# Starting twelve expert blocks ahead of the final block table, earlier row loads, and two PSUM banks each for turned rows and output

## What is computed

```python
x = x + attn(layernorm(x))              # causal self-attention, 16 heads of 8
x = x + xattn(layernorm(x), ctx, ctx)   # cross-attention without a softmax, own layernorm on its result
x = x + ffn(layernorm(x))

def ffn(x):                             # 8 experts, 128 -> 512 -> 128
    assign = argmax(x @ centroids.T)    # one expert for each token
    xn = xhat * ln_g[e] + ln_b[e]
    h = relu(xn @ w1[e].T + b1[e])
    y = x + h @ w2[e].T + b2[e]
    a = sigmoid((x @ centroids.T)[e])
    return a * y + (1 - a) * x          # for the token's expert e
```

## Time and profile before

| what | value |
|---|---|
| median of 3 runs | 640.61 us (639.78 to 641.74) |
| the profiled execution's own time | 648.02 us |
| its span in the profile | 646.2 us |
| TensorE busy | 553.8 us (86%) |
| VectorE busy | 516.4 us (80%) |
| POOL busy | 486.3 us (75%) |
| ScalarE busy | 429.3 us (66%) |
| mean granted TensorE clock | 0.954 of full speed |

### The profile page before, as it was taken

The page is one execution under the profiler, slowest core; times in us unless marked ns, Lnnn a source line. Parts: engine busy times, 40 slices in busy tenths (PEclk is TensorE's granted clock), DMA queues, the critical chain, the costliest instruction groups (busy, mean ns, idle before and its releaser), DMA issues. The chain is left out here.

```text
span 646.2 us, 24863 instructions
## 1 busy us (share of the span) xinstructions
PE 553.8 (86%) x7908; PEld 421.4 (65%) x7940; DVE 516.4 (80%) x1852; ACT 429.3 (66%) x1127; POOL 486.3 (75%) x891
## 2 busy tenths in 40 slices
PE   1647999999999999999999999986329989899993
PEld 0434676766666666666666666654219989898893
DVE  1567799899999999999998999887557767676673
ACT  1534777877787877778787777763217777677771
POOL 1412478888888889888888888787826888887885
PEclk9877999999999999999999999999559999999998
DMA  8300112311221131111112111100021222221220
GB/s 156 96 8 26 44 44 63 91 52 52 69 85 52 56 95 55 52 56 50 36 40 65 37 36 40 41 24 20 18 66 52 70 59 65 61 70 52 65 63 9
DMA packets 55183, 35.35 MB, mean 55 GB/s; under 512 B 14977, under 2 KB 50434, under 8 KB 55057
## 3 DMA queue, kind: packets, MB, share of 16 engines
q1 hardware_dynamic: 49584, 24.16, 14.1%
q0 software_dynamic: 4320, 8.66, 3.9%
q10 hardware_dynamic: 1152, 0.94, 0.5%
HBM read 24.46 MB, written 9.74 MB: 53 GB/s over the span
## 5 line engine op out<-in xcount | busy, mean ns | idle before, releaser
L1753 POOL DMA_INDIRECT out<-yo,rb x71 | 74.3, 1046 | 23.1 <-issue 11.7
L962 ACT ACTIVATE prob<-quad 128x1024 f32<-128x1024 f32 x64 | 62.1, 1021 | 35.1 <-PE quad L679 35.1
L869 PE MATMUL quad<-w,hT 128*128 x568 | 78.0, 281 | 6.5 <-DVE yb L1556 5.0
L946 ACT ACTIVATE ex<-qk,cf 128x512 f32<-128x512 f32 x128 | 81.9, 718 | 0.0
L1712 POOL DMA_INDIRECT expert_rows<-pay,sli x64 | 65.7, 1026 | 20.1 <-issue 15.5
L1279 DVE TENSOR_REDUCE mx<-quad 128x16 f32<-128x1024 f32 x64 | 75.2, 1216 | 5.2 <-PE quad L644 4.6
L869 PEld LDWEIGHTS quad<-w,hT 128*128 128x128 f32 x568 | 69.8, 193 | 9.9 <-issue 9.3
L1747 POOL TENSOR_SCALAR bs<-rb 128x128 f32<-128x128 f32 x71 | 58.7, 826 | 10.5 <-DMA rb<-expert_rows 6.8
L1538 DVE TENSOR_SCALAR xh<-rb 128x128 f32<-128x128 f32 x71 | 28.7, 404 | 40.2 <-DMA rb<-expert_rows 25.7
L679 PE MATMUL quad<-ex,qk 32*64 32x256 f32 x1024 | 47.3, 396 | 4.4 <-issue 4.0
L1071 ACT ACTIVATE xhT<-quad,gb 128x128 f32<-128x128 f32 x71 | 32.5, 458 | 24.9 <-PE quad L844 18.3
(11 more groups left out here) (220 smaller groups left out, 1625.0 us busy)
## 6 DMA issues: line engine op xcount, KB each, us to landing
rb<-expert_rows SPq DMA_DIRECT2D x71, 68.0 KB
xin<-in_x SPq DMA_DIRECT2D x32, 128.0 KB, 2.5
cin<-in_ctx SPq DMA_DIRECT2D x32, 128.0 KB, 3.1
xr<-in_x SPq DMA_DIRECT2D x32, 128.0 KB, 2.2
w<-in_w1t SPq DMA_DIRECT2D x8, 256.0 KB, 3.5
w<-in_w2t SPq DMA_DIRECT2D x8, 256.0 KB, 3.4
out<-yo,rb POOLq DMA_INDIRECT x71
expert_rows<-pay,sli POOLq DMA_INDIRECT x64
```

The source lines that it names most:

```text
L869: last = mm(M[1][:, 0:D], hT[u][:, c, :], w2[:, bass.ds(e, 1), c, :], start=c == 0, stop=c == FC - 1)
L946: act(ex[g.par][:, i, :, :].rearrange("p a t -> p (a t)"), qk[g.par][:, :, :].rearrange("p a t -> p (a t)"), ACT.Copy, scale=own4[:, i:i + ...
L962: act(prob[g.par][:, 2 * h_:2 * h_ + 2, :], quad[:, 2 * h_:2 * h_ + 2, :], ACT.Exp).then_inc(*ac_a.done(f"e{h_}"))
L1753: v.indirect_dma_start(out=o_rows, out_offset=bass.IndirectOffsetOnAxis(ap=number, axis=0), in_=yo[b.c % 4][:, :], in_offset=None, bounds_ ...
```

## The change

- Row loads: x of group g is loaded in round g of SP's program, ctx in round g + 2 and the residual in round g + 3. `late_loads` keep their rounds.
- After `counted` of group 11 the counts are kept (`te`). 12 groups of 256 tokens hold at least 12 full blocks of 128. In round 33 VectorE computes a table of the first NB1 = 12 blocks from them (`early_table`), all full ones, and signals `s_tab` the first time. The preparations stand in round 9.
- SP fetches blocks 0 to 7 after its last row load, once the early table and the scatters of the first 12 groups are there. All eight pad writes are then on SP, followed by the fetches of blocks 8 to 11; from block 12 on it waits for the pads, the final table and all scatters.
- `rows_in` of blocks 0 and 1 is in VectorE's round 37; TensorE does `transposed` of 0 and 1 and `hidden` of 0 in round 38, after `ranks` of group 30 and before that of group 31.
- The final table leaves out the blocks already used and is computed in ten pieces in VectorE's blocks 1 to 5 (`last_table`), with the running sum as one masked reduction.
- Turned rows have banks 0 and 1, outputs banks 4 and 5. `transposed` and `second` lose their waits for the block before; `hidden` always waits for `act_xT` and `second` for `dve_relu`.

```diff
@@ -150,6 +150,9 @@
     NG = NT // J
     CAP = T + P
     NBLK = NT + E - 1
+    NB1, GT = 12, 12
+    NB2 = NBLK - NB1
+    assert RB <= NB1 and NB1 * P <= GT * TG - E * (P - 1)
     x_rows = x.rearrange("b s d -> (b s) d")
     c_rows = ctx.rearrange("b s d -> (b s) d")
     o_rows = out.rearrange("b s d -> (b s) d")
...
@@ -310,6 +325,7 @@
         side = es.enter_context(nc.psum_tensor("side", [P, 4, 512], FP32))
         bank = [quad[:, i, :] for i in range(4)] + [side[:, i, :] for i in range(4)]
         M = bank[0:2]
+        XT, YB = bank[0:2], bank[4:6]
         HT = [bank[2:4], bank[6:8]]
         def stage_steps(name, pieces):
...
@@ -504,24 +523,14 @@
                              ).then_inc(d_c[g.par], 16)
             def one(g):
-                stage(g, 6, load_ctx)
-                stage(g, 7, load_again)
-                stage(g, 4, load_x)
+                stage(g, 2, load_ctx)
+                stage(g, 3, load_again)
+                stage(g, 0, load_x)
             rounds(nc.sync, one, early=late_loads)
             sp.wait_ge(s_padt, 1)
             sp.dma_start(rows[E * CAP:E * CAP + P, :], padt[:, :]).then_inc(d_pad, 16)
-            sp.wait_ge(s_pads, 1)
-            for e in range(E // 2):
-                at = nc.sync.value_load(pri[0:1, e:e + 1], min_val=0, max_val=(e + 1) * CAP - P)
-                sp.dma_start(rows[bass.ds(at, P), :], padt[:, :]).then_inc(d_pad, 16)
-            sp.wait_ge(d_pad, 16 * (E + 1))
-            sp.wait_ge(s_tab, 1)
-
-            sp.wait_ge(d_s[0], 16 * J * ((NG + 1) // 2))
-            sp.wait_ge(d_s[1], 16 * J * (NG // 2))
-
             def fetch(b):
                 if b.c >= RB:
...
@@ -530,7 +539,24 @@
                 at = nc.sync.value_load(bti[0:1, 1, bass.ds(b.n, 1)], min_val=0, max_val=E * CAP)
                 sp.dma_start(rb[b.c % RB][:, :], rows[bass.ds(at, P), :]).then_inc(d_rb[b.c % RB], 16)
-            for c in range(NBLK):
+
+            sp.wait_ge(s_tab, 1)
+            sp.wait_ge(d_s[0], 16 * J * ((GT + 1) // 2))
+            sp.wait_ge(d_s[1], 16 * J * (GT // 2))
+            for c in range(RB):
+                fetch(Block(c))
+            sp.wait_ge(s_pads, 1)
+            for e in range(E):
+                at = nc.sync.value_load(pri[0:1, e:e + 1], min_val=0, max_val=(e + 1) * CAP - P)
+                sp.dma_start(rows[bass.ds(at, P), :], padt[:, :]).then_inc(d_pad, 16)
+            for c in range(RB, NB1):
+                fetch(Block(c))
+
+            sp.wait_ge(d_pad, 16 * (E + 1))
+            sp.wait_ge(s_tab, 2)
+            sp.wait_ge(d_s[0], 16 * J * ((NG + 1) // 2))
+            sp.wait_ge(d_s[1], 16 * J * (NG // 2))
+            for c in range(NB1, NBLK):
                 fetch(Block(c))
             for i in range(4):
...
@@ -827,21 +853,19 @@
                 stage(g, 2, values)
                 stage(g, 4, weighted, 1)
-            rounds(nc.tensor, one)
-
-
-            wait(pe, dv_r, NG - 1, "tot")
-
             def expert(b):
+
+                if b.c == NB1:
+                    pe.wait_ge(s_tab, 2)
                 return nc.tensor.value_load(bti[0:1, 0, bass.ds(b.n, 1)], min_val=0, max_val=E - 1)
             def transposed(b):
+
                 if b.c < 4:
                     wait_b(pe, "dve_xh", b.n)
-                wait_b(pe, "act_xT", b.n - 1)
-                tr(M[0][:, 0:P], xh[b.c % 2][:, :], identf).then_inc(*ffn["pe_xT"].done("pe_xT"))
+                tr(XT[b.c % 2][:, 0:P], xh[b.c % 2][:, :], identf).then_inc(*ffn["pe_xT"].done("pe_xT"))
             def hidden(b):
...
@@ -850,7 +874,7 @@
                 if b.c < 2:
                     wait_b(pe, "act_w1", b.n)
-                if b.c == NBLK - 1:
+                else:
                     wait_b(pe, "act_xT", b.n)
                 for c in range(FC):
                     last = mm(HT[u][c // 2][:, (c % 2) * P:(c % 2 + 1) * P], w1b[u][:, c * P:(c + 1) * P],
...
@@ -862,35 +886,33 @@
                 u = b.c % 2
                 wait_b(pe, "act_relu", b.n)
-                if b.c == 0:
-                    wait_b(pe, "dve_relu", b.n)
-                wait_b(pe, "dve_yb", b.n - 1)
+                wait_b(pe, "dve_relu", b.n)
                 for c in range(FC):
-                    last = mm(M[1][:, 0:D], hT[u][:, c, :], w2[:, bass.ds(e, 1), c, :],
+                    last = mm(YB[u][:, 0:D], hT[u][:, c, :], w2[:, bass.ds(e, 1), c, :],
                               start=c == 0, stop=c == FC - 1)
                 last.then_inc(*ffn["pe_y"].done("pe_y"))
+            def first_blocks(i):
+
+                if i == TOTAL - 2:
+                    transposed(Block(0))
+                    transposed(Block(1))
+                    hidden(Block(0))
+
+            rounds(nc.tensor, one, early=first_blocks)
+
+
             pe.wait_ge(s_tab, 1)
-
...
-            transposed(Block(0))
-            transposed(Block(1))
-            steps([Block(c) for c in range(NBLK + 1)])
+            e1 = expert(Block(0))
+            transposed(Block(2))
+            for c in range(1, NBLK + 1):
+                if c < NBLK:
+                    hidden(Block(c))
+                second(Block(c - 1), e1)
+                if c < NBLK:
+                    e1 = expert(Block(c))
+                if c + 2 < NBLK:
+                    transposed(Block(c + 2))
         @block.scalar
...
@@ -1058,17 +1080,13 @@
             ac.wait_ge(d_late, 16 * N_LATE)
             ac.wait_ge(d_weights, 16 * N_WEIGHTS)
-            ac.wait_ge(s_pads, 1)
-            for e in range(E // 2, E):
-                at = nc.scalar.value_load(pri[0:1, e:e + 1], min_val=0, max_val=(e + 1) * CAP - P)
-                ac.dma_start(rows[bass.ds(at, P), :], padt[:, :]).then_inc(d_pad, 16)
             ac.wait_ge(s_tab, 1)
             def turned(b, e):
                 wait_b(ac, "pe_xT", b.n)
-                act(xhT[b.c % 2][:, :], M[0][:, 0:P], ACT.Identity, scale=gb[:, 0, bass.ds(e, 1)],
+                act(xhT[b.c % 2][:, :], XT[b.c % 2][:, 0:P], ACT.Identity, scale=gb[:, 0, bass.ds(e, 1)],
                     bias=gb[:, 1, bass.ds(e, 1)]).then_inc(*ffn["act_xT"].done("act_xT"))
             def relu(b, e):
...
@@ -1432,6 +1453,11 @@
                 wait(dv, dv_r, g.n, "rk")
                 v.tensor_tensor(cnt[:, :], cnt[:, :], BANK["ranks"][:, J * E:(J + 1) * E], ALU.add
                                 ).then_inc(*dv_r.done("tot"))
+                if g.n == GT - 1:
+                    wait(dv, dv_r, g.n, "tot")
+                    dv.wait_ge(s_early, 1)
+                    v.scalar_tensor_tensor(te[:, :], cnt[:, :], -float(P - 1), over[:, :], ALU.add, ALU.add
+                                           ).then_inc(s_early, 1)
             def own_rank(g):
...
@@ -1480,8 +1506,66 @@
                 stage(g, 0, stats_x)
                 stage(g, 4, own_head)
+            def early_table():
+
+
+                one_ = (P, NB1, E)
+                g1, n1 = geb[:, 0:NB1, :], gnb[:, 0:NB1, :]
+                dv.wait_ge(s_early, 2)
+                v.tensor_scalar(te[:, :], te[:, :], 7, None, ALU.logical_shift_right).then_inc(s_early, 1)
+                dv.wait_ge(s_early, 3)
+                v.tensor_copy(full[:, :], te[:, :]).then_inc(s_early, 1)
+                dv.wait_ge(s_early, 4)
+                v.tensor_tensor(below[:, :, :], upto[:, :, :], full[:, :].unsqueeze(1).broadcast_to((P, E, E)),
+                                ALU.mult).then_inc(s_early, 1)
+                v.tensor_scalar(step_e[:, :], full[:, :], -float(P), float(CAP), ALU.mult, ALU.add)
+                dv.wait_ge(s_early, 5)
+                v.tensor_reduce(cum1[:, :], below[:, :, :], AX.X, ALU.add).then_inc(s_early, 1)
+                dv.wait_ge(s_early, 6)
+                v.tensor_tensor(g1, blkno[:, 0:NB1].unsqueeze(2).broadcast_to(one_),
+                                cum1[:, :].unsqueeze(1).broadcast_to(one_), ALU.is_ge).then_inc(s_early, 1)
+                v.tensor_scalar(least[:, :], cum1[:, :], float(NB1), None, ALU.min).then_inc(s_early, 1)
+                dv.wait_ge(s_early, 7)
+                v.tensor_tensor(n1, g1, step_e[:, :].unsqueeze(1).broadcast_to(one_), ALU.mult).then_inc(s_early, 1)
+                v.tensor_reduce(bex[:, 0:NB1], g1, AX.X, ALU.add).then_inc(s_early, 1)
+                dv.wait_ge(s_early, 9)
+                v.tensor_reduce(bst[:, 0:NB1], n1, AX.X, ALU.add).then_inc(s_early, 1)
+                dv.wait_ge(s_early, 10)
+                v.tensor_copy(bti[:, 0, 0:NB1], bex[:, 0:NB1])
+                dv.wait_ge(s_early, 11)
+                v.tensor_tensor(bti[:, 1, 0:NB1], bst[:, 0:NB1], row_k[:, 0:NB1], ALU.add).then_inc(s_tab, 1)
+                v.tensor_copy(used[:, 0:1], least[:, 0:1])
+                v.tensor_tensor(used[:, 1:E], least[:, 1:E], least[:, 0:E - 1], ALU.subtract).then_inc(s_early, 1)
+                dv.wait_ge(s_early, 12)
+                v.tensor_tensor(skip_e[:, :], used[:, 1:E + 1], used[:, 0:E], ALU.subtract).then_inc(s_early, 1)
```

(80 more changed lines are left out.)

95 lines of the change are left out of this document (38 added, 57 removed).

## The result

| | before | after |
|---|---|---|
| median, same chip, 4 runs each | 641.14 us (639.78 to 641.74) | 634.96 us (632.32 to 635.61) |
| ratio after to before, 95% interval | | 0.9899 (0.9865 to 0.9932) |
| profiled execution, its span | 648.02, 646.2 us | 635.28, 633.4 us |

The change makes the kernel 6.5 us faster by the ratio (0.0101 x 641.14; interval 4.4 to 8.7), 6.2 by the medians. Forecast were 7.5. The two profiled spans differ by 12.8 us, twice that. So the traces are compared stretch by stretch and the total is taken from the medians.

The account below looks back on a forecast made before the run. TensorE and VectorE were taken as nearly full in routing, POOL fullest in the blocks, with late loads at the start and a hole between stages. Seven terms sum to -7.5 us, from the 640.6 median to 633.1 (630.5 to 635.5).

Parts of the forecast that it names:

- Term 1: Start: first ctx rows reach TensorE at 11.8 us instead of 19.8, -8.0 us (-6.4 to -8.8).
- Term 2: Routing stage: five added VectorE ops in rounds 9 and 19, +0.5 us (0 to +0.95).
- Term 3: Round 33: early table's eighteen VectorE instructions take 3.2 us ahead of row_max of group 30, +2.7 us (0 to +4.0).
- Term 4: Round 37: rows_in of blocks 0 and 1 ahead of choose of group 30, +0.5 us (0 to +0.7).
- term 5: Start of the blocks: out(0) at 482.5 us instead of 489.19, -6.7 us (-4.7 to -8.8).
- Term 6: Blocks 1 to 5: the final table's thirteen VectorE instructions, 4.3 us, mostly show, +4.0 us (+2.5 to +4.3).
- Term 7: Block stage: with two banks each, second no longer waits for the previous block's yb, -0.5 us (0 to -2).
- A: Rival: the twelve early blocks pay as well, later idle hiding table work, 628.9 us; chance 0.17.
- B: Rival: TensorE's slow clock lasts through the first blocks, +4.4 us, 637.5 us; chance 0.13.
- C: Rival: the mask load blocks the row loads behind it, ending slower, +2, some 643 us; chance 0.03.
- D: Rival: the loads give nothing because something else sets the start, 8 us less gain, 641 us; chance 0.07.

Follow-up runs that it names:

- after_again: The kernel after, unchanged, run again on the third chip: 633.58 us, ratio 0.9903 to before.
- before_again: The kernel before, unchanged, run again on the first group's chip: 646.22 us, ratio 0.9977 to before.
- table_late: The kernel after with the early table three rounds later, in round 36: 630.69 us, ratio 0.9874 to before.
- hidden_after: The kernel after with hidden of block 0 behind TensorE's rounds, so after the last ranks: 632.13 us, ratio 0.9884 to before.
- no_loads: The kernel after with its three row loads back in rounds 4, 6 and 7: 649.60 us, ratio 1.0040 to before.
- table_in_hole: hidden_after with the whole final table ahead of block 0's relu on VectorE, instead of in blocks 1 to 5: 628.64 us, ratio 0.9828 to before.
- loads_only: The kernel before with only the three row loads four rounds sooner: 639.57 us, ratio 0.9884 to before.

## Why the prediction was right, and where its terms were off

The forecast of 633.1 us, in its own range of 630.5 to 635.5, met 634.96. The mechanism is the one forecast: the loads make the gain, and what the early blocks win is lost to the two tables. That the total came so near is in part luck, since the errors of terms 3 to 6 have opposite signs. The terms one by one:

**Term 1, -8.0:** right. -8.57 for the first ctx rows in the trace, -7.5 (-9.4 to -5.7) for the loads alone.

**Term 2, +0.5:** not tried by itself. The stretch from round 4 to 33 in the kernels with early loads and the new operations is not longer than before.

**Term 3, +2.7:** the step that was mis-sized. "12 x 0.22 + 6 x 0.10 = 3.2" takes each instruction at its own length; three were held by POOL's operations and the table took 4.68. From round 33 to 35 the kernel after takes 3.0 us more than before (27.1 and 24.2), `after_again` 4.7 more than `before_again`; the mean of the five kernels with the table there is 28.2 and of the nine without 23.5, so 4.7 is the better figure, above the bound of +4.0 that was given. The fall of TensorE's clock was in no term. In all five it is at the lower level there, in none of the other nine: for 3.4 us in the kernel after and for 6.8 in the four others, whose stretch is 1.2 to 1.9 us longer. By an estimate from these differences, taken as even over the time, 6.8 us at the lower level cost 2.3 to 3.8 us, so about half or more of the 4.7 would be the clock. No run parts the two: `table_late` removes both.

**Term 4, +0.5, and term 5, -6.7:** out(0) starts 39.9 us after `own_head` of round 35, and 44.9 before, so -5.0 where -6.2 was forecast (-5.4 for `after_again` against `before_again`). From the end of ScalarE's rounds (459.30) to out(0) the trace takes 13.1 us, the prediction's steps 12.6: right but for the two expert numbers, 1.35 with no work beside them. The order itself has a price that the term took as given: by `hidden_after`, `hidden` ahead of the last `ranks` costs 2.0 us. The other 1.2 us are lost before that end, where `rows_in` of blocks 0 and 1 stands in round 37 (26.8 us after `own_head` of round 35, and 25.6 before). That is term 4, above its bound of +0.7; but `before_again` takes 26.1 and `no_loads`, which has the two `rows_in`, 26.1 as well, so their price was not shown alone.

**Term 6, +4.0:** out(5) comes 13.4 us after out(0), 10.5 before: +2.9; it is +2.1 for `after_again` against `before_again`, and `table_in_hole` gives 2.5 by the outs and 3.5 by the times. The sign and the place are right, the size is nearer the low bound of +2.5 than the +4.0.

**Term 7, -0.5:** POOL's idle for yo is 10.0 us in eight waits in the kernel after, against 11.5 in five. Nothing of the term shows behind out(5) (140.3 us, and 139.3 before).

Together, from round 33 to out(5): 80.5 us in the kernel after and 81.5 in `after_again`, against 79.6 and 80.1. That is +0.9 and +1.4, where terms 3 to 6 gave +0.5. In the second pair term 3 is 2.0 us dearer than forecast, terms 4 and 5 bring 0.8 less, and term 6 costs 1.9 less: they nearly cancel, and nothing in the working made them do so; `no_loads` with +2.6 is on the same side.

**The rivals.** A (the early blocks pay): no, they cost, by the 27.1 us of rounds 33 to 35 and by `no_loads`. B (the slow clock lasts): no; the clock is 0.77 from 470 to 475 and 1.00 from 475, while VectorE's table still puts holes between the blocks. The Trainium skill, "TensorE: Matmul & The Clock Gate", "HAM oscillation — how this bites in real kernels", describes matmul groups that are throttled again each time, where the wait between two groups is longer than the work of one. The waits between these blocks are not like that (0.76 us, with TensorE busy for 4.24 of 5), so it does not speak for B, and the clock stayed at 1.00. C (the mask): no wait on rows behind the load at 21.95. D (the loads give nothing): `loads_only` rules it out.

**What stays open.** From round 4 to 33 every kernel that has both the early loads and the rest of the change takes 364 to 368 us, and each of the other five 369 to 372. It can't be the loads alone (371.1) nor the rest alone (371.7). The two sets differ in kind as well: in the nine, a median round takes 12.2 to 12.3 us and `y_sum` waits 0.01 us on average, in the five 12.5 to 12.7 us and 0.3 to 0.4. But four of the five ran on the chip where before takes 646.68 us, and the fifth is the execution that is 6.9 above its median, about what this stretch differs by. No trace shows the kernel before in an execution near 641 us. So chip and execution can explain it as well as a gain that needs both parts. The sum of the parts by their ratios is -7.5 + 2.6 = -4.9, against -6.5 for the whole. The 1.6 us between them would be room for such a gain, but it is smaller than what the three intervals leave open.

## What to carry to other kernels

Work that is moved ahead pays only as far as the engine that comes last in its chain is moved with it: `hidden` inside the rounds started no sooner, and held up what stood behind it by 2.0 us, until ScalarE's turned rows and weights were put ahead too (55.3 to 49.2 us). Small serial work belongs where its engine waits for another one anyway: the same thirteen table instructions cost 2.5 us between the first outs, and 0.5 us in the hole ahead of them (3.5 us between the two by the times). Times of two traces are compared from a mark that both share, such as `own_head` of the same round, and not from the start of the span. And when VectorE instructions are put into a full pipeline, look at what POOL does at that moment, not only at their lengths.
